# Edge stage of a graph-attention kernel: two operands of VectorE moved to PSUM, and the carried row added in two parts

## The chip, the cores and the metric

The kernel runs on one core of one Trainium2 chip. The metric is the device time of one launch in microseconds; the kernel before took 2041.8 us (median of three runs, 2036.73 to 2044.93).

## The reference

A graph-attention layer over N = 6250 nodes and E = 100000 edges, with a residual, and then a small network on the normalised result, again with a residual. The edges come sorted by `dst`. Cut to what matters:

```python
h = leaky_relu(layernorm(x) @ W.T + b)            # 6250 x 512, as 8 heads of 64
e_src, e_dst = sum(h * w_att_src), sum(h * w_att_dst)
e  = leaky_relu(e_src[src] + e_dst[dst])          # one score per edge and head
ex = exp(e - segment_max(e, dst)[dst])
a  = ex / segment_sum(ex, dst)[dst] * edge_attr_8
msg = h[src] * a[:, :, None]                      # 100000 x 512
x  = x + segment_sum(msg, dst)
x  = x + ffn(layernorm(x))                        # a decoder with two tiny networks
```

Everything is computed in float32; some operands are split into three bfloat16 parts that add up to the float32 value.

## The kernel before

Four stages run one after the other. `project` computes `h` and the scores for 49 tiles of 128 nodes and stores rows of 520 numbers (512 of `h` and 8 scores) in the HBM table `table_h`. `prepare` computes the node windows. `attend_windows` is the edge stage and holds the whole change. `finish` divides, normalises and runs the network.

The edge stage works on 112 groups of 7 x 128 = 896 edges. As `dst` is sorted, the edges of a group end in a window of 128 nodes that begins at the group's base. For a group g (slot s = g mod 3 of the triple buffers):

- ScalarE copies the 896 source node numbers to `src_idx` (`set_src`), and GpSimd issues seven indirect DMAs (L768), each of which gathers 128 rows of `table_h` into `gathered`. GpSimd does nothing else in this stage. It may refill a slot when the messages of three groups before are made (L766).
- VectorE, `make_member` (L778): compares the node numbers 0 to 127 (`node_no`, in SBUF) with the edges' place in the window (`rel`, in SBUF) and writes the 0/1 matrix `member16`, 128 x 896. TensorE transposes it (L872), ScalarE copies it widened to float32 (`widen_member`) and copies the transpose from PSUM (`turn_member`), both at L907.
- TensorE, `at_edges` (L863): fetches the destination scores of each edge by a product with the transposed matrix.
- VectorE, `scores` (L786 to L798): waits for the seven gathers, adds the scores. ScalarE takes the exponential (L919).
- VectorE, `messages`: L803 multiplies the exponentials by the edge attributes into `coef`, 128 x 56, in SBUF; L810 multiplies `gathered` (128 x 3584) by `coef`, each coefficient repeated over 64 columns, into `msg`.
- TensorE, `add_up` (L885): seven float32 products of `member` and `msg` accumulate the group's 128 x 512 sums in one of the PSUM banks 0 to 2 (each product is two matmul records), and L892 the sums of the exponentials in bank 3.
- ScalarE, `evacuate`, copies the sums to `summed`; VectorE, `evacuate_weights` (L830), the sums of the exponentials behind them.
- Windows overlap. So before the window is stored, SP loads the first row of it, as the groups before left it in `table_agg`, to `carry` (L752), VectorE adds it to row 0 of `summed` (`carry_in`, L840, one instruction of 1 x 520), and SP stores the 128 x 520 window (L741). The load waits until the store of the group before has landed.

Each engine has its own order, written out by hand as rounds: `stage(u, slot, lag, do)` runs step `do` for group u - lag in round u. VectorE's round is, in this order: `carry_in` (lag 4), `scores` (1), `make_member` (0), `weights_parts` (1), `messages` (1), `weights_last_part` (1), `evacuate_weights` (3). TensorE's is `at_edges` (1), `add_up` part 0 with three of seven products (2), `transpose` (0), `add_up` part 1 (2). SP's is window load (0), carry load (4), store (4). Rounds 0 to 8 and the last few are unrolled, those between run in a hardware loop of three rounds a pass. An engine waits in order: what stands behind a waiting instruction on its queue waits too.

Of the kernel before, what the change touches and what calls it, by code (L numbers as in the profile page):

```python
# [18 lines left out]
ALU = mybir.AluOpType  # L19
# [627 lines left out]
def attend_windows(nc, top, banks, t, keep, branch_semaphores):  # L647
# [6 lines left out]
    with ExitStack() as ctx:  # L654
# [22 lines left out]
        ex_rest = sb("w_ex_rest", [P, GROUP, HEADS])  # L677
        coef = sb("w_coef", [P, GROUP, HEADS])
        msg = sb("w_msg", [P, S3, GROUP, D])
# [4 lines left out]
        member_t = banks[4][:, :].bitcast(BF16)  # L684
        edge_dst = banks[6]

        s_no = sem("node_no_loaded")
        s_pool_on = sem("w_pool_went_on")
        s_i16 = sem("ident16_set")
# [32 lines left out]
        with nc.Block() as block:  # L722
            @block.sync
            def _(sp):
# [8 lines left out]
                def store(g, s):  # L733
                    base = sp.value_load(keep["bases_int"][0:1, bass.ds(g, 1)], min_val=0, max_val=NODES)
                    if isinstance(g, int) and g == 0:
                        sp.wait_ge(d["evac"], 1)
                        sp.wait_ge(d["evac_w"], 1)
                    else:

                        sp.wait_ge(d["carried"], g)  # L740
                    sp.dma_start(t["agg"][bass.ds(base, P), :], summed[:, s, :]).then_inc(s_put[s], 48)  # L741

                def load_carry(g, s):

                    if isinstance(g, int) and g == 0:
                        return
                    base = sp.value_load(keep["bases_int"][0:1, bass.ds(g, 1)], min_val=0, max_val=NODES)
                    if reused(g):
                        sp.wait_ge(d["carried"], g - 1)
                    before = (s - 1) % S3  # L750
                    sp.wait_ge(s_put[before], filled(g - 1, before, 48))
                    sp.dma_start(carry[:, :], t["agg"][bass.ds(base, 1), :]).then_inc(s_carry, 16)  # L752
# [21 lines left out]
            def _(dve):  # L774
                def make_member(g, s):
                    if old(g):
                        dve.wait_ge(d["sums"], g - 2)
                    nc.vector.tensor_tensor(  # L778
                        member16[:, s, :, :], node_no[:, :].unsqueeze(1).to_broadcast([P, GROUP, P]),
                        keep["rel"][:, bass.ds(g * GROUP, GROUP)].unsqueeze(2).to_broadcast([P, GROUP, P]),  # L780
                        ALU.is_equal).then_inc(d["member16"], 1)
# [19 lines left out]
                def messages(g, s):  # L801
                    dve.wait_ge(d["ex"], g + 1)
                    nc.vector.tensor_tensor(coef[:, :, :], ex[:, s, :, :],  # L803
                                            keep["dist"][:, bass.ds(g * GROUP, GROUP), :], ALU.mult
                                            ).then_inc(d["coef"], 1)
                    dve.wait_ge(d["coef"], g + 1)
                    if old(g):
# [4 lines left out]
                        gathered[:, s, :, 0:D].rearrange("p j (h d) -> p j h d", h=HEADS),  # L812
                        coef[:, :, :].unsqueeze(3).to_broadcast(shape), ALU.mult).then_inc(d["msg"], 1)

# [19 lines left out]
                def carry_in(g, s):  # L834
                    if isinstance(g, int) and g == 0:
# [3 lines left out]
                    dve.wait_ge(s_carry, 16 * g)  # L839
                    nc.vector.tensor_tensor(summed[0:1, s, :], summed[0:1, s, :], carry[:, :], ALU.add  # L840
                                            ).then_inc(d["carried"], 1)

                dve.wait_ge(s_no, 16)
                for u, slot in rounds(dve, 4):
                    stage(u, slot, 4, carry_in)
# [8 lines left out]
            def _(pe):  # L854
# [21 lines left out]
                def add_up(g, s, part):  # L876
                    if part == 0:
                        pe.wait_ge(d["msg"], g + 1)
                        pe.wait_ge(d["member"], g + 1)
                        if old(g):  # L880
                            pe.wait_ge(d["evac"], g - 2)
                    half = GROUP // 2
                    for j in range(half) if part == 0 else range(half, GROUP):
# [621 lines left out]
```

## Time and profile before

| | us |
|---|---|
| three runs | 2036.73, 2041.8, 2044.93 |
| median | 2041.8 |
| span of the profiled execution | 2022.8 |
| busy: PE / DVE / ACT / POOL | 1448.3 / 1285.9 / 488.2 / 1282.9 |
| mean granted TensorE clock | 0.864 of full speed |

PE is TensorE (PEld its weight loads), DVE is VectorE, ACT is ScalarE, POOL is GpSimd, SP is the engine that issues the plain DMAs (SPq its queue). The span runs from the first to the last instruction of one profiled execution; its device time is not listed apart from the three runs. An engine counts as busy while an instruction of its own runs, and that includes time in which the instruction is held up by something outside it. The edge stage takes the span from about 354 us to about 1738 us.

### The profile page before, as it was taken

What the parts mean: (1) busy time and instruction counts of PE and PEld (TensorE: products, weight loads), DVE (VectorE), ACT (ScalarE), POOL (GpSimd) and SP (SyncE); (2) the same over time, 40 slices, a digit from 0 to 9 for tenths busy, and PEclk for the clock granted to TensorE, in tenths of its full rate; (3) what the DMA queues carried; (4) which work ended last, traced back from release to release, by engine and by line L of the source; (5) the groups of instructions that cost most, each with busy time, mean ns of one, the idle gap of its engine ahead of it and who ended that gap; (6) DMA issues with size and microseconds to landing.
All of it is one profiled execution on the core that took longest, in us unless ns stands there. A gap on an engine that the chain in (4) does not pass through costs nothing. (4 is left out here: it accounts for less than half of the span.)

```text
span 2022.8 us, 23283 instructions
## 1 busy us (share of the span) xinstructions
PE 1448.3 (72%) x5502; PEld 680.4 (34%) x5502; DVE 1285.9 (64%) x2420; ACT 488.2 (24%) x1141; POOL 1282.9 (63%) x932
## 2 busy tenths in 40 slices
PE   5878782476677667677767677677676777189998
PEld 2333331233333233333333333333333333045555
DVE  5777875465665666655566555556665555588884
ACT  1222220222222222222222222222222222033332
POOL 1222221888888888888888888888888887023341
PEclk9899996688988988978797888888878888689988
DMA  6333333566566666566666556666655665325441
GB/s 222 126 126 126 126 126 65 158 179 180 174 175 179 185 177 175 170 179 176 180 179 176 170 170 181 179 176 178 177 171 171 180 180 164 121 105 187 169 154 67
DMA packets 151399, 326.43 MB, mean 161 GB/s; under 512 B 47313, under 2 KB 47569, under 8 KB 151247
## 3 DMA queue, kind: packets, MB, share of 16 engines
q0 software_dynamic: 62720, 208.78, 36.5%
q1 hardware_dynamic: 88654, 117.38, 16.9%
q8 instruction: 9, 0.15, 0.0%
q14 instruction: 16, 0.12, 0.0%
HBM read 255.82 MB, written 70.27 MB: 161 GB/s over the span
## 5 line engine op out<-in xcount | busy, mean ns | idle before, releaser
L768 POOL DMA_INDIRECT gathered<-table_h,w_src_idx x784 | 1121.0, 1430 | 256.4 <-issue 256.4
L885 PE MATMUL bank<-w_msg,member 128*128 128x512 f32 x1568 | 880.1, 710 | 1.8 <-DVE w_msg L810 1.8
L885 PEld LDWEIGHTS bank<-w_msg,member 128*128 128x128 f32 x1568 | 341.8, 231 | 367.3 <-issue 365.4
L810 DVE TENSOR_TENSOR w_msg<-gathered,w_coef 128x3584 f32<-128x3584 f32 x112 | 435.9, 3892 | 3.9
L786 DVE TENSOR_REDUCE at_dst<-bank 128x112 f32<-128x336 f32 x112 | 56.9, 508 | 525.2 <-DMA gathered<-table_h,w_src_idx 525.2
L872 PE MATMUL bank<-ident,member 128*128 128x128 bf16 x784 | 83.3, 265 | 421.6 <-DVE member L778 421.6
L919 ACT ACTIVATE w_ex<-w_diff 128x56 f32<-128x56 f32 x112 | 27.9, 249 | 967.8 <-DVE w_diff L798 967.8
L208 POOL TENSOR_TENSOR prod_dst<-hrow,w_dst 128x512 f32<-128x512 f32 x49 | 75.6, 1543 | 247.1 <-DVE hrow L237 247.1
L872 PEld LDWEIGHTS bank<-ident,member 128*128 128x128 bf16 x784 | 58.7, 117 | 513.4 <-DVE member L778 478.1
L277 PE MATMUL bank<-wt,xnT 128*128 128x512 f32 x392 | 199.7, 657 | 0.0
L1113 POOL TENSOR_TENSOR res<-x_in,y 128x2048 f32<-128x2048 f32 (+1 forms) x13 | 63.4, 4880 | 197.0 <-DMA out<-res 136.7
L1196 PE MATMUL bank<-h,w 128*128 128x512 f32 (+1 forms) x338 | 162.4, 625 | 0.0
L778 DVE TENSOR_TENSOR member<-node_no,k_rel 128x896 bf16<-128x896 f32 x112 | 121.8, 1087 | 10.6 <-DMA node_no<-in_node_no 10.6
L907 ACT ACTIVATE member<-member 128x896 f32<-128x896 bf16 x112 | 106.4, 950 | 64.6 <-DVE member L778 64.6
L277 PEld LDWEIGHTS bank<-wt,xnT 128*128 128x128 f32 x392 | 76.9, 206 | 93.6 <-issue 93.6
L907 ACT ACTIVATE memberT<-bank 128x896 bf16<-128x896 bf16 x112 | 100.7, 899 | 0.1
L840 DVE TENSOR_TENSOR summed<-summed,w_carry 1x520 f32<-1x520 f32 x111 | 76.4, 688 | 26.6 <-DVE summed L830 20.4
L286 PE MATMUL bank<-ident,xn 128*128 128x128 f32 x196 | 32.4, 289 | 78.3 <-DVE xn L227 78.3
L1196 PEld LDWEIGHTS bank<-h,w 128*128 128x128 f32 x338 | 64.0, 208 | 58.9 <-issue 56.9
L1142 ACT ACTIVATE h<-bank,b 128x512 f32<-128x512 f32 (+1 forms) x65 | 41.7, 661 | 133.3 <-PE bank L1196 67.1
L1207 PEld LDWEIGHTS bank<-w,h 128*128 128x128 f32 x490 | 64.5, 205 | 16.8 <-issue 16.1
L907 ACT ACTIVATE summed<-bank 128x512 f32<-128x512 f32 x112 | 65.8, 588 | 11.0 <-PE bank L892 11.0
(133 smaller groups left out, 1155.2 us busy)
## 6 DMA issues: line engine op xcount, KB each, us to landing
table_agg<-summed SPq DMA_DIRECT2D x112, 260.0 KB
table_agg<-zeros SPq DMA_DIRECT2D x50, 260.0 KB, 2.2
table_h<-hrow SPq DMA_DIRECT2D x49, 260.0 KB, 2.1
xt<-in_x SPq DMA_DIRECT2D x49, 256.0 KB, 2.7
gathered<-table_h,w_src_idx POOLq DMA_INDIRECT x784
agg_in<-table_agg SPq DMA_DIRECT2D x12, 1040.0 KB, 7.6
x_in<-in_x SPq DMA_DIRECT2D x12, 1024.0 KB, 5.5
out<-res SPq DMA_DIRECT2D x12, 1024.0 KB, 4.4
```

Of the source, the lines that this page charges most:

```text
L208: nc.gpsimd.tensor_tensor(prod_dst[:, s, :], hrow[:, s, 0:D], w_dst[:, :], ALU.mult).then_inc(s_pdst, 1)
L277: mm = nc.tensor.matmul(ps_h[s][:, :], xnT[:, s, c * P:(c + 1) * P], wt[:, c, :], start=False, stop=(c == DC - 1))
L768: pool.indirect_dma_start(out=gathered[:, s, j, :], out_offset=None, in_=t["h"][:, :], in_offset=bass.IndirectOffsetOnAxis(ap=src_idx[:, s ...
L778: nc.vector.tensor_tensor(member16[:, s, :, :], node_no[:, :].unsqueeze(1).to_broadcast([P, GROUP, P]), keep["rel"][:, bass.ds(g * GROUP, ...
L810: nc.vector.tensor_tensor(msg[:, s, :, :].rearrange("p j (h d) -> p j h d", h=HEADS), gathered[:, s, :, 0:D].rearrange("p j (h d) -> p j h ...
L840: nc.vector.tensor_tensor(summed[0:1, s, :], summed[0:1, s, :], carry[:, :], ALU.add).then_inc(d["carried"], 1)
L872: last = nc.tensor.transpose(member_t[:, j * P:(j + 1) * P], member16[:, s, j, :], ident16[:, :])
L885: nc.tensor.matmul(sums[s][:, :], member[:, s, j, :], msg[:, s, j, :], start=first, stop=final)
L907: return nc.scalar.activation(out, in_, ACT.Copy)
L1113: nc.gpsimd.tensor_tensor(res[:, s, 0:k, :], x[:, s, 0:k, :], y[:, s, 0:k, :], ALU.add).then_inc(d["res"], 1)
L1196: last = nc.tensor.matmul(bank[:, 0:w], w2[:, weights, :], h1[:, units, 0:w], start=(i == 0), stop=(i == len(pairs) - 1))
L1207: last = nc.tensor.matmul(y3[:, 8 * j:8 * j + 8], h2[:, g, j * P:(j + 1) * P], w3[:, g, :], start=(g == 0), stop=(g == 4))
```

## The change

The edge stage's `coef` and node numbers move from SBUF to PSUM banks 5 and 7, which the stage did not use. The node numbers are copied there once, by VectorE, before the rounds begin. `carry_in` becomes two instructions: the first adds `carry` to row 0 of the sums as they stand in their PSUM bank and writes columns 0 to 511 of row 0 of `summed`; the second adds the last eight columns as before. Each increments the semaphore `carried`, so it now counts two a group, and the waits on it are doubled. TensorE gets one more wait: before it overwrites a sums bank it waits for the `carry_in` of the group that had that bank. All other code is the same.

```diff
-        coef = sb("w_coef", [P, GROUP, HEADS])
+        coef = banks[5][:, 0:GROUP * HEADS].rearrange("p (j h) -> p j h", h=HEADS)
+        node_row = banks[7][:, 0:P]
+        s_row = sem("node_row_set")
@@ store(g, s), on SP
-                        sp.wait_ge(d["carried"], g)
+                        sp.wait_ge(d["carried"], 2 * g)
@@ load_carry(g, s), on SP
-                        sp.wait_ge(d["carried"], g - 1)
+                        sp.wait_ge(d["carried"], 2 * (g - 1))
@@ make_member(g, s), on VectorE
-                        member16[:, s, :, :], node_no[:, :].unsqueeze(1).to_broadcast([P, GROUP, P]),
+                        member16[:, s, :, :], node_row.unsqueeze(1).to_broadcast([P, GROUP, P]),
@@ messages(g, s), on VectorE
-                    nc.vector.tensor_tensor(coef[:, :, :], ex[:, s, :, :],
+                    nc.vector.tensor_tensor(coef, ex[:, s, :, :],
                                             keep["dist"][:, bass.ds(g * GROUP, GROUP), :], ALU.mult
                                             ).then_inc(d["coef"], 1)
...
                         gathered[:, s, :, 0:D].rearrange("p j (h d) -> p j h d", h=HEADS),
-                        coef[:, :, :].unsqueeze(3).to_broadcast(shape), ALU.mult).then_inc(d["msg"], 1)
+                        coef.unsqueeze(3).to_broadcast(shape), ALU.mult).then_inc(d["msg"], 1)
@@ carry_in(g, s), on VectorE
-                    nc.vector.tensor_tensor(summed[0:1, s, :], summed[0:1, s, :], carry[:, :], ALU.add
+                    nc.vector.tensor_tensor(summed[0:1, s, 0:D], sums[s][0:1, :], carry[:, 0:D], ALU.add
                                             ).then_inc(d["carried"], 1)
+                    nc.vector.tensor_tensor(summed[0:1, s, D:ROW], summed[0:1, s, D:ROW], carry[:, D:ROW], ALU.add
+                                            ).then_inc(d["carried"], 1)
 
                 dve.wait_ge(s_no, 16)
+                nc.vector.tensor_copy(node_row, node_no[:, :]).then_inc(s_row, 1)
+                dve.wait_ge(s_row, 1)
@@ add_up(g, s, part), on TensorE, part 0
                             pe.wait_ge(d["evac"], g - 2)
+                            if reused(g, S3 + 1):
+                                pe.wait_ge(d["carried"], 2 * (g - 3))
```

## Rows read from the trace of the kernel before

**Rows 1.** The page: busy time and shares by engine; POOL's busy tenths in 40 slices.
```profile
PE 1448.3 (72%) x5502; PEld 680.4 (34%) x5502; DVE 1285.9 (64%) x2420; ACT 488.2 (24%) x1141; POOL 1282.9 (63%) x932
POOL 1222221888888888888888888888888887023341
```
**Rows 2.** Stages: window, us, busy us of PE, PEld, DVE, ACT, POOL, clock, DMA, GB/s.
```profile
1000.00:1300.00 300.00, 212.63 (x873) 97.40 (x874) 179.64 (x271) 74.02 (x174) 247.73 (x172) 0.87 0.60 175
```
**Rows 3.** Waits from 440 to 1690 us: us in total, times, longest us.
```profile
DVE at_dst L786 <- DMA gathered<-table_h,w_src_idx: 471.0, 103, 5.7
```
**Rows 4.** Order of time, POOL: start us, us; first and last of 784 gathers.
```profile
354.49 1.82 POOL L768 DMA_INDIRECT gathered<-table_h,w_src_idx  x1 [17.77 <-issue]
...
1713.14 0.95 POOL L768 DMA_INDIRECT gathered<-table_h,w_src_idx  x1 [0.30 <-issue]
```
**Rows 5.** Order of time, DVE and POOL, one round of the loop.
```profile
1010.04 0.51 DVE L786 TENSOR_REDUCE at_dst<-bank 128x112 f32<-128x336 f32 x1 [4.19 <-DMA gathered<-table_h,w_src_idx]
...
1011.35 1.09 DVE L778 TENSOR_TENSOR member<-node_no,k_rel 128x896 bf16<-128x896 f32 x1
...
1012.11 1.16 POOL L768 DMA_INDIRECT gathered<-table_h,w_src_idx  x1 [0.30 <-issue]
...
1012.73 3.89 DVE L810 TENSOR_TENSOR w_msg<-gathered,w_coef 128x3584 f32<-128x3584 f32 x1
...
1013.57 3.88 POOL L768 DMA_INDIRECT gathered<-table_h,w_src_idx  x1 [0.30 <-issue]
...
1017.04 0.69 DVE L840 TENSOR_TENSOR summed<-summed,w_carry 1x520 f32<-1x520 f32 x1 [0.20 <-DVE summed L830]
...
1017.75 0.94 POOL L768 DMA_INDIRECT gathered<-table_h,w_src_idx  x1 [0.30 <-issue]
```
**Rows 6.** Order of time, a gather beside a reduction that reads PSUM alone.
```profile
416.86 0.51 DVE L786 TENSOR_REDUCE at_dst<-bank 128x112 f32<-128x336 f32 x1 [5.00 <-DMA gathered<-table_h,w_src_idx]
416.99 0.95 POOL L768 DMA_INDIRECT gathered<-table_h,w_src_idx  x1 [0.30 <-issue]
```
**Rows 7.** Order of time, the projection's POOL and DVE products side by side.
```profile
103.00 1.26 POOL L208 TENSOR_TENSOR prod_dst<-hrow,w_dst 128x512 f32<-128x512 f32 x1 [5.69 <-DVE hrow L237]
...
108.89 0.69 DVE L241 TENSOR_TENSOR prod_src<-hrow,w_src 128x512 f32<-128x512 f32 x1
...
108.94 1.77 POOL L208 TENSOR_TENSOR prod_dst<-hrow,w_dst 128x512 f32<-128x512 f32 x1 [4.68 <-DVE hrow L237]
...
109.62 0.69 DVE L244 TENSOR_REDUCE hrow<-prod_src 128x8 f32<-128x512 f32 x1
```
**Rows 8.** Lines L237 and L241: duration ns min/median/max, first and last start.
```profile
L237 DVE TENSOR_TENSOR hrow<-leak,bank x49: 677/686/690, 27.5 to 321.5; 128x512 f32<-128x512 f32 x49
L241 DVE TENSOR_TENSOR prod_src<-hrow,w_src x49: 691/692/1733, 28.2 to 322.2; 128x512 f32<-128x512 f32 x49
```
**Rows 9.** Groups of DVE, 460 to 1690 us: busy us, mean ns of one.
```profile
L803 DVE TENSOR_TENSOR w_coef<-w_ex,k_dist 128x56 f32<-128x56 f32 x101 | 21.1, 209 | 0.0
L830 DVE TENSOR_REDUCE summed<-bank 128x8 f32<-128x24 f32 x101 | 17.7, 175 | 0.0
```
**Rows 10.** Order of time, SP's queue and DVE: a store, carry loads, one awaited.
```profile
1006.03 0.42 SPq L741 DMA_DIRECT2D table_agg<-summed  x1
...
1009.34 0.28 SPq L752 DMA_DIRECT2D w_carry<-table_agg  x1
...
1728.08 0.28 SPq L752 DMA_DIRECT2D w_carry<-table_agg  x1
...
1729.86 0.69 DVE L840 TENSOR_TENSOR summed<-summed,w_carry 1x520 f32<-1x520 f32 x1 [4.14 <-DMA w_carry<-table_agg]
```
**Rows 11.** Order of time, PE: the products of two rounds.
```profile
1012.91 3.65 PE L885 MATMUL bank<-w_msg,member 128*128 128x512 f32 x8
...
1017.30 2.82 PE L885 MATMUL bank<-w_msg,member 128*128 128x512 f32 x6
...
1025.21 5.12 PE L885 MATMUL bank<-w_msg,member 128*128 128x512 f32 x8
```

## The prediction

> **What bounds the kernel now.** I read the page first. PE has the largest share, 72% of the span, but POOL stands at 8 tenths in every slice of the edge stage and at 1 to 4 elsewhere [rows 1], and the change lies in that stage alone. The stage's window row says more: in 300 us of it POOL is busy 247.73, PE 212.63, DVE 179.64, and the 16 DMA engines at 0.60 [rows 2]. Who waits for whom settles it: VectorE waits for the gathers 103 times in 103 rounds, 471.0 us in all [rows 3]. So the gathers come last, and everything behind them has slack.
>
> In the order of time POOL rests only 0.30 us between two gathers [rows 5]. 784 gathers start between 354.49 and 1713.14 us [rows 4]: 1358.65 / 783 = 1.735 us each, 12.15 us for a group of seven. An undisturbed one takes 0.95 + 0.30 = 1.25 us [rows 5]; seven would be 8.75. The missing 3.40 us are in two gathers of each round [rows 5]. One starts at 1013.57, while L810 runs from 1012.73 to 1016.62, and lasts 3.88 us instead of 0.95: it ends 0.83 us after L810 does. The other starts at 1012.11 inside L778 (to 1012.44) and lasts 1.16: it ends 0.83 us after L778 does. Two events with one law: a gather that needs something 0.12 us after its start gets it only when the VectorE instruction is through, and then needs 0.83 us more. Both instructions have two inputs in SBUF. A gather that starts inside L786, which reads PSUM alone, takes 0.95 [rows 6]: it isn't held. The projection shows the same of POOL's own arithmetic [rows 7]: L208 takes 1.26 us when it goes first, and 1.77 when it starts 0.05 us after L241 with its two SBUF inputs; L244, one SBUF input, runs inside that same L208 for its usual 0.69 and adds nothing. So two SBUF inputs hold GpSimd up, and one or none doesn't.
>
> **The change part by part.**
>
> *L810 reads `coef` from PSUM.* It then has one SBUF input. By the law above the blocked gather loses 3.88 - 0.95 = 2.93 us in every round. No row shows an instruction with one SBUF and one PSUM input beside a working GpSimd; the bounds are 0 (blocks as now) and 2.93 (does not). I take 2.93, as L244 with one SBUF input and L786 with a PSUM input both let GpSimd work.
>
> The Trainium skill, "SBUF — State Buffer", section "Who interferes with whom", says so outright: a Vector instruction with two SBUF inputs contends with a GpSimd instruction that reads SBUF, one with at most one SBUF input outside the two-port modes does not. The trace agrees as far as it goes (3.88 against 0.95 us).
>
> *L778 reads the node numbers from PSUM.* Likewise one SBUF input. Of the 3.40 us, 2.93 are L810's; the rest, 0.47 us a round on average, is L778's (0.21 in the round shown), and it goes too, between 0 and 0.47. I take all of it.
>
> *What still blocks.* Six VectorE instructions a round of some 0.21 us (L790, L793, L798, L818, L803 [rows 9], L823), and the new last part of `carry_in`, keep two SBUF inputs. A gather's critical instant falls into one of them with a chance of 0.21 / 1.25 and then waits 0.1 us on average: 7 x 0.017 = 0.12 us a round. So POOL needs 8.75 + 0.12 = 8.87 us a round (8.75 to 9.1).
>
> *VectorE's own time.* A round's chain goes from L786 at 1010.04 to the end of L840 at 1017.73: 7.69 us of 12.15 [rows 5]. L810, L778 and L840 change an operand to PSUM. L237, 128 x 512 with one input in PSUM, takes 686 ns, and L241 with both in SBUF 692 when undisturbed [rows 8]: 0 us each. Both operands are read repeatedly (64 columns a coefficient, seven times the node row); no row shows that from PSUM, nearest is L786, which walks 336 elements of PSUM with a stride in 0.51 us [rows 6] where L237 needs 0.69 for 512, so the same slope. I take 0; the other bound is a doubled rate, which is a rival below. L803 writes to PSUM: its 209 ns [rows 9] could become 0.1 us more or less. `carry_in` becomes 512 columns (0.68, as L237) plus eight (0.175 as L830 [rows 9], to 0.21): +0.17 to +0.2 us. Sum: 7.9 us, up to 8.2. That is under 8.87, so it is hidden, but the cover shrinks from 4.2 us to 0.7 to 1.0 us: if VectorE's round grew beyond 8.87 each 0.1 us would cost 11 us.
>
> The Trainium skill, "VectorE: DVE Perf Modes", section "The TRN2 errata", gives 120 fixed cycles for a PSUM source against 58 for an SBUF one. By that three instructions a round would cost 65 ns more each, 0.2 us, and VectorE's round would be 8.1 us, still under POOL's. The row on L237 shows no such cost, and the row decides.
>
> *The new wait on TensorE* (part 0 of `add_up` g for `carry_in` g - 3). Queued behind it are all products, the transposes, and through them VectorE. But the same place already waits for the messages of g, which VectorE makes in the same round as `carry_in` g - 3 and 6 us later. It costs 0.
>
> *The doubled count on SP.* The store waits for the second part: 0.2 us later. Behind it on SP's queue stand the next window load, the carry load and the next store. Store to carry load is 3.3 us, the load's landing about 1.8 (1728.08 to 1729.86, where VectorE waited for it) [rows 10], `carry_in` with its handover about 1.1: some 6.2 us of 8.87. Cost 0, cover 2.6 us, from which slower transfers would take.
>
> *The copy of the node numbers*: once, at most 0.5 us.
>
> *Sum.* 783 x (1.735 - 8.87 / 7) = 783 x 0.468 = 366 us. Fill and drain around the 784 gathers, and the stages before and after, stay. Span 2022.8 - 366 = 1657; around it lie 19 us (2041.8 - 2022.8), so 1676 us for a run like the median.
>
> **What is late next.** Three things come close to 8.87 us a round.
> DMA: 0.60 x 12.15 = 7.3 us of all 16 engines a round [rows 2], a share of 0.82 afterwards. PE: 212.63 / 300 x 12.15 = 8.6 us a round, but at a mean clock of 0.87 [rows 2]. Eight records took 3.65 us in one round and 5.12 in the next [rows 11], after products had ended at 1020.12 and PE had stood nearly idle for over 4 us. At the full clock (2.4 GHz) the work is 8.6 x 0.87 = 7.5 us. With a round of 8.87 only about 1.4 us of idleness is left, so I expect the clock to rise. VectorE: 7.9.
>
> **The rivals.**
> (a) *TensorE or the DMA engines become the bound.* If the clock stays at 0.87 and PE keeps some 0.6 us of waits (for L778's output and L830), the round is 8.6 + 0.6 = 9.2 us; if packets stretch by a third under the denser load, 7.3 becomes 9.8. For: both would stand at over 0.8. Against: neither is at its limit on average, and the three slots let POOL run up to two groups ahead of a late round. Times: 9.2 gives 2041.8 - 112 x 2.95 = 1711; 9.8 gives 1779.
> (b) *The lock doesn't care where the second input lies.* Any two-input instruction, PSUM or not, holds GpSimd. Then POOL's 12.15 stays, and the 0.2 us more on VectorE are hidden: 2042. For: no row shows the mix. Against: rows 6 and 7.
> (c) *Slower: PSUM delivers a repeated operand at half the rate.* An element costs 1.045 ns ((3.89 - 0.69) / (3584 - 520), rows 5), so L810 would take 3.75 us more and L778 0.94; VectorE's round is then 7.69 + 0.2 + 4.69 = 12.58 us, and it, not POOL, is the bound: 112 x 0.43 = +48 us, 2090. It decides from the point where the two take over 4.26 us more in sum. Against: L237 and L786 at the usual rate.
>
> **How the numbers follow.** Forecast (round 8.75 to 9.1) 0.66, rival (a) 0.22, (b) 0.08, (c) 0.04. Range: from 8.7 us a round, 1656, up into rival (a) at 9.8 us, 1780; that leaves out (b), (c) and the far end of (a), about 0.17. Less than 0.5% (10 us) can't be told from no change with this kernel. Faster 0.88, same 0.08, slower 0.04.
>
> **What would show it.** In the new profile no gather should last over 1.2 us, the mean of a gather should fall from 1.43 (1.735 - 0.30) to about 0.97 us, and POOL's tenths should fall slightly while its gathers come every 1.27 us. L810 should stay at 3.89 and L778 at 1.09. VectorE's wait for the gathers should shrink from 4.5 us to under 1 a round, and PE's clock should rise above 0.9. I am wrong if gathers of 3.9 us are still there (b), if L810 is longer (c), or if POOL shows waits for `msg` or VectorE waits for TensorE instead of the gathers (a).

## The result, and the profile after

The changed kernel took 2155.1 us (median of 4, 2149.2 to 2164.6) where the kernel before takes 2042.8 (4 runs, 2036.7 to 2044.9): ratio 1.058, 95% interval 1.052 to 1.063. The forecast was 1676 us. Run again, unaltered, in two later sets of runs on two different chips, the changed kernel took 2111.6 us in one and **1664.9 us** in the other, each beside runs of the kernel before at 2045.5 and 2039.0. The record names the chips of the later sets, but not that of the first measurement, nor the one on which the kernel before was profiled. So this section shows two profiles of one program: "the first" is that of the 2155 us, "the later" that of the 1665 us. Line numbers are those of the changed kernel: L770 is the gather, L812 the messages, L780 the member comparison, L788 the first reduction of a round, L842 and L844 the carried row, L743, L733 and L754 SP's store, window load and carry load.

The pages, first and then later: busy time and shares, and POOL's and the DMA engines' tenths of 40 slices.

```profile
PE 1415.2 (66%) x5502; PEld 665.2 (31%) x5502; DVE 1289.2 (60%) x2532; ACT 493.6 (23%) x1141; POOL 902.0 (42%) x932
POOL 1222223554645545545545445445445454122331
DMA  5333335565645645655555555555555455324441
```
```profile
PE 1327.7 (80%) x5502; PEld 617.2 (37%) x5502; DVE 1294.2 (78%) x2532; ACT 488.4 (29%) x1141; POOL 905.2 (54%) x932
POOL 1222222237777777777777777777777712133341
DMA  6433343258888888888888888888888843244431
```

POOL's busy time fell from 1282.9 us [rows 1] to 902 in the first and 905 in the later: the hold of GpSimd by VectorE is gone in both. What is left is spread differently: 7 tenths in nearly every slice of the stage in the later profile, 4 to 6 in the first one, where POOL now waits. The 300 us windows of [rows 2] say it again, first and then later (busy us of PE, PEld, DVE, ACT, POOL, then clock, DMA share, GB/s):

```profile
1000.00:1300.00 300.00, 189.35 (x803) 86.01 (x804) 167.67 (x277) 69.89 (x163) 148.32 (x157) 0.83 0.56 159
```
```profile
1000.00:1300.00 300.00, 252.53 (x1196) 112.07 (x1194) 249.44 (x410) 101.22 (x238) 227.14 (x240) 1.00 0.83 244
```

The gathers (duration in ns min/median/max, first and last start) and what POOL waited for, in the first profile and then in the later one:

```profile
L770 POOL DMA_INDIRECT gathered<-table_h,w_src_idx x784: 940/946/1297, 353.9 to 1825.0; - x196
its engine sat idle before it (us, times) until:
  DVE w_msg L812: 359.6, 35
  issue: 235.6, 711
  ACT w_src_idx L915: 152.7, 38
```
```profile
L770 POOL DMA_INDIRECT gathered<-table_h,w_src_idx x784: 942/949/1297, 357.4 to 1339.5; - x196
its engine sat idle before it (us, times) until:
  issue: 227.0, 690
  ACT w_src_idx L915: 28.7, 94
DMA to landing us min/median/max: 3.5/3.9/4.9
```

No gather lasts 3.9 us any more in either. But in the first profile POOL stood still 35 times until VectorE's messages had freed a slot, 359.6 us in all, and VectorE in turn waited before L788 (first, then later):

```profile
L788 DVE TENSOR_REDUCE at_dst<-bank x112: 487/506/509, 365.5 to 1835.2; 128x112 f32<-128x336 f32 x112
its engine sat idle before it (us, times) until:
  remote: 419.7, 38
  PE bank L869: 72.4, 33
```
```profile
L788 DVE TENSOR_REDUCE at_dst<-bank x112: 507/508/509, 369.0 to 1344.4; 128x112 f32<-128x336 f32 x112
its engine sat idle before it (us, times) until:
  DMA gathered<-table_h,w_src_idx: 139.5, 112
```

"Remote" is a release for which the trace has no event at the right time. Before, this wait was for the gathers [rows 3]; in the later profile it still is, 1.2 us a time. In the first one most of it is for TensorE, which had long been done. The second round shows it best, since up to it the two executions do the same. Order of time, first profile:

```profile
368.84 0.91 ACT L915 ACTIVATE memberT<-bank 128x896 bf16<-128x896 bf16 x1
...
369.80 0.46 PE L869 MATMUL bank<-window,memberT 128*128 128x48 bf16 x7 [1.01 <-ACT memberT L915]
...
379.06 0.51 DVE L788 TENSOR_REDUCE at_dst<-bank 128x112 f32<-128x336 f32 x1 [6.95 <-remote]
...
381.38 0.93 PE L878 MATMUL bank<-ident,member 128*128 128x128 bf16 x7 [3.85 <-issue]
...
393.81 0.92 ACT L915 ACTIVATE memberT<-bank 128x896 bf16<-128x896 bf16 x1 [11.36 <-remote]
```

and later profile:

```profile
372.31 0.91 ACT L915 ACTIVATE memberT<-bank 128x896 bf16<-128x896 bf16 x1
...
373.28 0.46 PE L869 MATMUL bank<-window,memberT 128*128 128x48 bf16 x7 [1.01 <-ACT memberT L915]
...
377.72 0.51 DVE L788 TENSOR_REDUCE at_dst<-bank 128x112 f32<-128x336 f32 x1 [2.13 <-DMA gathered<-table_h,w_src_idx]
...
380.12 0.55 PE L878 MATMUL bank<-ident,member 128*128 128x128 bf16 x7
...
381.01 0.90 ACT L915 ACTIVATE memberT<-bank 128x896 bf16<-128x896 bf16 x1
```

The seven L869 end at 370.26 in the first profile. The semaphore that VectorE waits for is recorded as raised at 378.97, 8.7 us later (later profile: products end at 373.74, raised at 373.75). Not all of that is lost, as VectorE also needs the gathers: it stood idle 6.95 us instead of 2.13. L878's products end at 382.31, and ScalarE starts on them at 393.81, 11.5 us later (later profile: 0.34 us). This is all or nothing: in 35 of the 112 rounds of the first profile L788 starts 12.0 to 13.1 us after the end of its L869 products, in 68 under 1 us. The gathers' transfers, by contrast, aren't late: from the start of a gather to the end of its last packet it is 3.76 us in the median of the first profile and 3.85 in the later one. A third thing is late: SP. Its own register instructions and DMA issues, which take 0.02 to 0.5 us elsewhere, take 0.70 us each in many cases while gathers stream. In the first profile, order of time on SP's queue and POOL:

```profile
1029.03 0.95 POOL L770 DMA_INDIRECT gathered<-table_h,w_src_idx  x1 [0.30 <-issue]
1029.34 0.71 SPq L743 DMA_DIRECT2D table_agg<-summed  x1
...
1032.79 0.95 POOL L770 DMA_INDIRECT gathered<-table_h,w_src_idx  x1 [0.30 <-issue]
1036.39 0.00 SPq L733 DMA_DIRECT2D window<-table_shifts  x1
1036.65 0.51 DVE L788 TENSOR_REDUCE at_dst<-bank 128x112 f32<-128x336 f32 x1 [11.51 <-remote]
...
1043.99 0.95 POOL L770 DMA_INDIRECT gathered<-table_h,w_src_idx  x1 [10.26 <-DVE w_msg L812]
```

Between the store at 1029.34 and the window load at 1036.39 SP waits for nothing that is late; it works through its register instructions (start us, us; the first three took 0.03 to 0.04 us each at 1018.4 us, ahead of a slow stretch):

```
1034.28 0.697  L732 register arithmetic
1034.98 0.697  L733 wait for edge_dst, by a register
1035.68 0.698  L733 move
1036.39 0.002  L733 DMA issue
```

The last gather is issued at 1032.79, SP's slow stretch ends at 1036.39, and at 1036.65 VectorE wakes too, 12.6 us after the L869 products it waited for (1023.67 + 0.33). In the meantime POOL has used up its two groups of lead, and waits for VectorE in turn until 1043.99. That comes about once in three groups and makes the mean round (1824.99 - 353.90) / 783 x 7 = 13.15 us, against 12.15 before. POOL's two waits above, 359.6 + 152.7 us in 112 rounds, come to 4.6 us a round (the usual gaps of 0.30 us in them included); they are the difference to the 8.75 us that seven gathers take alone.

One number sorts the executions. The trace records each raise of a semaphore by a DMA queue ("landing"), here counted by stage, beside SP's register and issue instructions of 0.6 to 0.8 us between 354 and 1800 us (value loads left out):

```
                              landings, 0-345 us   whole run   slow SP instr.
kernel before (its profile)        2520             19823           0
the change, first profile          2520              7381         458
the change, later profile          2520             19832           0
```

Up to the first gather all agree; from there the first profile lacks most of the landings that the other two have, from the first group on. It also lacks some of the raises by engines: 4492 are recorded, against 5811 in the later profile of the same program.

### The profile page after: what moved, and what is told of

It is laid out like the page before. It is cut to its first block and busy times, and to the rows that moved or that the text cites. A ratio compares the mean times of both kernels' runs of the same rounds, so it can differ in the third digit from the quotient of the medians.

```text
span 2156.6 us, 23605 instructions
## 1 busy us (share of the span) xinstructions
PE 1415.2 (66%) x5502; PEld 665.2 (31%) x5502; DVE 1289.2 (60%) x2532; ACT 493.6 (23%) x1141; POOL 902.0 (42%) x932
## 5 line engine op out<-in xcount | busy, mean ns | idle before, releaser
L770 POOL DMA_INDIRECT gathered<-table_h,w_src_idx x784 | 741.5, 946 | 747.9 <-DVE w_msg L812 359.6
L893 PE MATMUL bank<-w_msg,member 128*128 128x512 f32 x1568 | 817.3, 667 | 1.8 <-DVE w_msg L812 1.8
L812 DVE TENSOR_TENSOR w_msg<-gathered,bank 128x3584 f32<-128x3584 f32 x112 | 435.3, 3887 | 3.8
L893 PEld LDWEIGHTS bank<-w_msg,member 128*128 128x128 f32 x1568 | 315.7, 214 | 324.4 <-issue 320.3
L878 PE MATMUL bank<-ident,member 128*128 128x128 bf16 x784 | 77.8, 253 | 508.1 <-DVE member L780 470.9
L788 DVE TENSOR_REDUCE at_dst<-bank 128x112 f32<-128x336 f32 x112 | 56.1, 501 | 511.1 <-remote 419.7
L878 PEld LDWEIGHTS bank<-ident,member 128*128 128x128 bf16 x784 | 56.5, 113 | 602.6 <-DVE member L780 481.5
L1204 PE MATMUL bank<-h,w 128*128 128x512 f32 (+1 forms) x338 | 175.0, 666 | 0.0
L842 DVE TENSOR_TENSOR summed<-bank,w_carry 1x512 f32<-1x512 f32 x111 | 75.3, 679 | 155.9 <-ACT summed L915 91.9
L780 DVE TENSOR_TENSOR member<-bank,k_rel 128x896 bf16<-128x896 f32 x112 | 121.6, 1085 | 0.0
L869 PE MATMUL bank<-window,memberT 128*128 128x48 bf16 x784 | 38.5, 185 | 74.7 <-ACT memberT L915 66.5
L1215 PEld LDWEIGHTS bank<-w,h 128*128 128x128 f32 x490 | 70.6, 221 | 21.1 <-issue 20.3
L1150 ACT ACTIVATE h<-bank,b 128x512 f32<-128x512 f32 (+1 forms) x65 | 41.6, 661 | 152.7 <-PE bank L1215 84.7
```

The lines of the kernel that those rows point to most:

```text
L770: pool.indirect_dma_start(out=gathered[:, s, j, :], out_offset=None, in_=t["h"][:, :], in_offset=bass.IndirectOffsetOnAxis(ap=src_idx[:, s ...
L780: nc.vector.tensor_tensor(member16[:, s, :, :], node_row.unsqueeze(1).to_broadcast([P, GROUP, P]), keep["rel"][:, bass.ds(g * GROUP, GROUP ...
L812: nc.vector.tensor_tensor(msg[:, s, :, :].rearrange("p j (h d) -> p j h d", h=HEADS), gathered[:, s, :, 0:D].rearrange("p j (h d) -> p j h ...
L842: nc.vector.tensor_tensor(summed[0:1, s, 0:D], sums[s][0:1, :], carry[:, 0:D], ALU.add).then_inc(d["carried"], 1)
L878: last = nc.tensor.transpose(member_t[:, j * P:(j + 1) * P], member16[:, s, j, :], ident16[:, :])
L893: nc.tensor.matmul(sums[s][:, :], member[:, s, j, :], msg[:, s, j, :], start=first, stop=final)
```

## The experiments

18 runs in six sets; all kernels of a set ran on one chip, and no two sets on the same. The expectations speak of theories: A, gathers that nothing holds up come too densely and keep wakings and SP back; B, the split carried row is the cost; C, the node numbers in PSUM; D, the load of the DMA engines; E and G, something else than the stream of gathers; H, the chip that a run is on. In the tables "landings" is the count of recorded landings in the run's profile, "slow SP" the count of SP instructions as above, and "round" is 7 x (last - first gather) / 783. Line numbers shift by a few between kernels.

### Set 1: the parts alone, and less lead

```diff
e1  coef in PSUM; node_no and the carried row as before
e2  node numbers in PSUM; coef and the carried row as before
e3  the carried row in two parts, with its waits; coef and node_no as before
e4  the whole change, and
-                        wait_alone(pool, d["msg"], g - 2, s_pool_on)
+                        wait_alone(pool, d["msg"], g - 1, s_pool_on)
```

> Of the change only the coefficients lie in PSUM; node numbers and the carried row are as before. Theory A (gathers that nothing holds up run too far ahead and too densely, and wakings by semaphores and SP's instructions then come late): the 3.89 us multiply no longer holds up a gather, so the gathers of a group run at 1.25 to 1.28 us and the stall comes as with the whole change: 2100 to 2170 us, SP instructions of 0.70 us in its records, gather rounds near 13 us. Theory B (the split carried row with its doubled count and TensorE's added wait is the cost): those are absent, so the gain forecast appears, 1680 to 1780 us. Theory C (the node numbers in PSUM are the cost): likewise 1700 to 1800 us.

> Only the node numbers lie in PSUM. Theory A: the held-up gather beside the member comparison goes from 1.16 to 0.95 us, 112 times 0.2 us, so at most 24 us of gain and no stall, as the multiply still holds up a gather each round: 2018 to 2045 us. Theory C: 2100 us or more. Theory B: 2018 to 2045 us.

> Only the carried row is added in two parts, the first read from PSUM, with the doubled count and TensorE's added wait. Theory A: nothing that holds up a gather goes, and the round is still GpSimd's 12.15 us: 2035 to 2050 us. Theory B (this is what costs): 2100 us or more. Theory C: 2035 to 2050 us.

> The whole change, and the gathers of group g wait for the messages of group g-2 instead of g-3, so that GpSimd runs at most one group ahead and pauses once a round instead of once in three rounds. Theory A: no long stretch of gathers without a pause, so the late wakings are short and the round becomes VectorE's 7.9 us plus the waits between the last landing of a group and its scores, or some 10 to 11 us: 1800 to 1920 us. Theory B or C (the split row, PSUM operands, or anything else in VectorE's or TensorE's chain): the pace of the gathers was not the limit, and one buffer less of lead makes it slower: 2155 to 2250 us.

```
              us (median)   ratio, 95% interval      landings   slow SP
e1 coef       2005.2        0.985 (0.980 to 0.989)     8809       202
e2 node       2026.2        0.994 (0.992 to 0.996)     9642         3
e3 carry      2036.2        0.998 (0.996 to 1.001)     9908        20
e4 less lead  2135.9        1.050 (1.044 to 1.057)     7343       365
```

e2 and e3 came as theory A had it, and show no cost of these two parts while the gathers are still held: 13 us of gain for e2, none for e3. e1 fell between: too slow for B and C, too quick for A, and its four runs lie wide apart (1992.8 to 2046.3). Its trace stalls as the change does, but still lets L778 hold up a gather now and then (a row of its waits, us in total, times, longest; and its gathers):

```profile
ACT memberT L907 <- remote: 267.4, 45, 9.3
...
L768 POOL DMA_INDIRECT gathered<-table_h,w_src_idx x784: 940/946/1869, 357.8 to 1656.9; - x196
```

Why holds of up to 0.9 us should bring 150 us against the whole change isn't settled. e4 missed the ranges of all theories: with one group less of lead the stall stays, and POOL, which was to pause briefly in each round, stops 72 times for 9.5 us in the median. All four have under 10,000 landings, e2 and e3 too, which kept the 3.9 us hold and didn't stall. They lack raises by engines too (4247 and 4437 recorded), so missing records alone don't make a kernel late.

### Set 2: spacing, bytes, rows, stores

```diff
e5  the whole change, behind each gather (pause is a new tile)
+                        wait_alone(pool, s_pause, g * GROUP + j, s_pool_on)
+                        nc.gpsimd.memset(pause[:, 0:8], 0.0).then_inc(s_pause, 1)
e6  in the 102 groups of the hardware loop: out=gathered[:, s, j, 0:260], rows of 260 columns read
e7  in the same 102 groups: out=gathered[0:64, ...], ap=src_idx[0:64, ...]
e8  in the 102 stores of the hardware loop: summed[:, s, 504:520] instead of all 520 columns
```

> The whole change, and behind each gather GpSimd writes 8 columns of a tile that nobody reads, and waits for that write before the next, so that the gathers start further apart than 1.25 us. Theory A (a stream of gathers with nothing between them keeps TensorE's and the DMA queues' wakings and SP's instructions back): with 0.1 to 0.3 us between gathers the 0.70 us SP instructions go or become rare, and a round costs 7 gathers of 1.4 to 1.55 us, 10 to 10.9 us: 1800 to 1900 us. Theory D (not the spacing, but the mean load of the DMA engines delays them): at a tenth or two less load little changes, 2080 to 2150 us. Theory E (the pace of the gathers is unrelated to the late wakings): 2155 us or more.

> The whole change, with gathers of 260 columns instead of 520 in all but the first nine groups (the tables' rows are then wrong ones, the count of gathers, of their rows and of their semaphore increments stays). Theory A (what matters is how densely GpSimd issues): same pace of issue, so the stall stays: 2100 to 2160 us and over 300 SP instructions of 0.70 us. Theory D (the bytes that the DMA engines move): the share of the engines in dense stretches falls from 0.8 to about 0.5 and the stall goes: 1670 to 1780 us.

> The whole change, with gathers of 64 rows instead of 128 in all but the first nine groups (half of the output rows of each are then stale); the count of gathers stays, bytes and row descriptors halve. If the number of descriptors written or moved is what delays, the stall goes: 1670 to 1780 us, or less if a gather of half the rows is also issued faster. If it is each gather's fixed part (its instruction, its increments from the 16 queues), the stall stays: 2100 us or more.

> The whole change, with stores of 16 columns instead of 520 in all but the first nine groups (the sums of a window are then not stored). Theory D (load of the DMA engines): 266 KB of 2.1 MB less a round, a gain of up to an eighth of the stall: 2000 to 2100 us; if the store's transfer was on the path of the carried row, the same. Theory A: 2130 to 2160 us, as the gathers are as dense as before.

```
                us (median)   ratio, 95% interval      landings   slow SP
e5 8 columns    2139.6        1.047 (1.044 to 1.051)     7342       423
e6 half bytes   2109.9        1.032 (1.026 to 1.037)     6823       384
e7 half rows    2122.7        1.038 (1.031 to 1.046)     7007       446
e8 small store  2134.8        1.044 (1.040 to 1.048)     7590       349
```

e5 tested nothing: the write fits into the gap that each gather leaves anyway, and the gathers still start 1.26 us apart (order of time of e5):

```profile
1012.54 0.96 POOL L772 DMA_INDIRECT gathered<-table_h,w_src_idx  x1 [0.18 <-POOL pause L778]
1013.50 0.12 POOL L778 MEMSET pause<- 128x8 f32 x1
1013.80 0.95 POOL L772 DMA_INDIRECT gathered<-table_h,w_src_idx  x1 [0.18 <-issue]
```

The other three leave out part of the data, so their results are not the layer's; their times tell what the transfers weigh. They rule out theory D: the DMA engines' tenths in the edge stage fall from 5 or 6 to 2 or 3 in e6 and e7, and neither half the bytes, nor half the rows, nor nearly no stores takes the stall away. They come 20 to 45 us under the change's first time, about as much as that kernel's own two stalled times differ (2155 and 2112).

### Set 3: real pauses, and the split row undone

```diff
e9   the whole change, once in each group
+                        if j == 3:
+                            if not (isinstance(g, int) and g == 0):
+                                wait_alone(pool, s_pause, g, s_pool_on)
+                            nc.gpsimd.memset(pause[:, 0:1560], 0.0).then_inc(s_pause, 1)
e10  the same with 3120 columns
e11  as e5 with 512 columns
e12  coef and node_row in PSUM, the carried row as before:
-                    nc.vector.tensor_tensor(summed[0:1, s, 0:D], sums[s][0:1, :], carry[:, 0:D], ALU.add
...
+                    nc.vector.tensor_tensor(summed[0:1, s, :], summed[0:1, s, :], carry[:, :], ALU.add
                                             ).then_inc(d["carried"], 1)
```

> The whole change, and once in each group, behind the fourth gather, GpSimd writes 1560 columns of a tile that nobody reads: by the 0.53 us of the 520 columns before (rows of L201) some 1.6 us. Theory A (what starves the wakings is an unbroken stream of gathers): a pause of 1.6 us every 8.75 us lets the late events through, the round is 8.75 + 1.4 = 10.2 us where the pause is long enough: 1800 to 1880 us; if 1.6 us doesn't suffice, 2050 to 2150 us. Theory G (the stream is not the cause; it is what VectorE's and TensorE's chains do with their operands in PSUM): 2155 us or more.

> The same with 3120 columns, some 3.2 us, about as long as the multiply of the kernel before held up a gather. Theory A: the round is 8.75 + 3 = 11.8 us with no stall, and few SP instructions of 0.70 us: 1980 to 2040 us, faster than the whole change although GpSimd is given more to do. Theory G: 2200 us or more, as GpSimd works longer and the stall stays.

> The whole change with 512 columns written behind each gather, some 0.5 us, of which 0.3 us lies in the gap that each gather leaves anyway: gathers start 1.45 to 1.55 us apart. Theory A with any small gap sufficing: a round of 10.2 to 10.9 us, 1800 to 1900 us. Theory A with a long gap needed: the stall stays at 2100 to 2160 us, and only the pauses help. Theory G: 2160 us or more.

> Coefficients and node numbers in PSUM, the carried row added as before, in one instruction with both operands in SBUF. Theory A: nothing of 3.9 or 1.1 us holds up a gather any more, the 0.69 us row of one partition at most: the stall stays, 2080 to 2160 us. Theory B (the split row and its waits make the stall once the gathers are fast): 1680 to 1900 us.

```
                 us (median)   ratio, 95% interval      landings   slow SP   round
e9  1.42 us      1801.4        0.884 (0.880 to 0.888)     19830        1     10.04
e10 2.72 us      1947.5        0.956 (0.947 to 0.964)     19799        2     11.34
e11 0.54 us x7   1986.1        0.975 (0.971 to 0.979)     19791        2     11.70
e12 no split     1661.8        0.817 (0.813 to 0.821)     19827        1      8.79
```

Three of the four missed their ranges: e10 came 32 us under its own, as the write took 2.72 us and not 3.2; e11 86 us over, as its gathers start 1.66 us apart and not 1.5; e12 18 us under that of theory B.

By these alone one would write: pauses cure the stall, and the split row is its cause, since e12 has no pause whatever between its gathers and is the quickest of all. The second is wrong, and the first isn't shown by this set. e12's first 16 us of the edge stage are the same instructions as the change's, no carried row has been touched by then, and yet the change's landings are already missing there. And all four of this set have their landings complete. What the four share isn't an edit but the chip, and the hour at which they ran.

### Set 4: the same three kernels on another chip

No edits: e13 is the changed kernel, e14 is e12, e15 is e9.

> The whole change, not altered, on this run's chip, beside two kernels that were fast on the chip before. Theory H (the late wakings belong to the chip that a run is on: the semaphore landings of the edge stage are recorded in full, some 19,800, on the chip on which all four kernels were fast, and 6,800 to 9,900 on the chips on which the others were slow, already in the first gathers, where the kernels do the same): on a chip with full landings the change runs at 1650 to 1690 us; on a chip with few, at 2140 to 2165 us. Theory B (the split row makes the stall): 2140 to 2165 us on every chip.

> The change without the split of the carried row, not altered from its first run. Theory H: 1650 to 1690 us on a chip with full landings, 2080 to 2165 us on one with few. Theory B: 1655 to 1675 us on every chip.

> The whole change with one pause of 1.6 us in each group, not altered from its first run. Theory H: 1795 to 1810 us on a chip with full landings; on one with few it says nothing of the pause: if the pause helps there, below 2050 us, if not, 2130 to 2180 us. Theory A with B (a pause mends the stall that the split row makes): 1795 to 1810 us on every chip.

```
                 us (median)   ratio, 95% interval      landings   slow SP   round
e13 the change   2111.6        1.033 (1.029 to 1.037)      7473      396     12.73
e14 as e12       2149.6        1.052 (1.048 to 1.056)      7094      370     12.90
e15 as e9        1920.4        0.940 (0.936 to 0.943)      8953      219     11.11
```

e13 stalls as theories B and H both had it, but 28 us under their range. e14 decides against the split row: one kernel, 1661.8 us in one set and 2149.6 in the other, 29% apart, while the kernel before stayed at 2036.8 and 2045.5. The kernel without the split row stalls too. The waits of L788 in e12 and in e14 (idle us, times, until):

```profile
  DMA gathered<-table_h,w_src_idx: 148.4, 112
```
```profile
  remote: 510.2, 49
  PE bank L867: 71.2, 49
```

e15 shows that a pause of 1.42 us in each group takes a large part of the stall away where there is one: a chip with few landings costs 1920 - 1801 = 119 us with it, against 2112 - 1665 = 447 without (e16 below). Of the three versions that ran on both kinds of chip it is the one that beat the kernel before on both, by 6% and by 12%.

### Sets 5 and 6: the change on a chip with full landings, and the long pause

No edits: e16 is the changed kernel, e17 and e18 are e10.

> The whole change, not altered, on whatever chip this set runs on. Theory H (the chip decides): with some 19,800 landings recorded 1650 to 1690 us, with under 10,000 recorded 2105 to 2165 us, and nothing between. If a chip with full landings gives 2100 us or more, the split row has a part in it after all.

> The whole change with one pause of 3.2 us in each group, not altered from its first run (1947.5 us, on the chip with full landings). On a chip with full landings 1930 to 1965 us again. On one with few: if a pause as long as the multiply's old hold lets all late wakings through, 1930 to 1975 us and under 30 SP instructions of 0.70 us; if the length of the pause is not what counts, a stall beside it, 2000 to 2150 us.

> The whole change with one pause of 3.2 us in each group, not altered (1946 and 1948 us in two sets, both on chips with full landings). On a chip with few landings: if a hold of 3 us a group, as the multiply gave in the kernel before, lets the late wakings through, 1935 to 1980 us and under 30 SP instructions of 0.70 us; if the hold is not what spared the kernel before, 2000 to 2150 us. On a chip with full landings 1930 to 1965 us, which would tell nothing new.

```
                 us (median)   ratio, 95% interval      landings   slow SP   round
e16 the change   1664.9        0.818 (0.809 to 0.827)     19832        0      8.78
e17 as e10       1946.2        0.956 (0.943 to 0.970)     19806        0     11.34
e18 as e10       1949.1        0.958 (0.948 to 0.968)     19798        0     11.34
```

e16 is the later profile shown above: the changed kernel itself is fast where the landings are complete, as theory H had it. e17 and e18 both fell on chips with full landings and repeat e10. Whether a pause of 2.7 us cures the stall on the other kind was not seen. That the kernel before didn't stall there, and e2 and e3 with its 3.9 us hold didn't, speaks for it. The kernel before has no profile from a set that stalled; that it runs on both kinds of chip is known by its times alone (medians of 2032.8 to 2045.5 over all sets).

The six sets fell three and three: full landings in sets 3, 5 and 6, few in sets 1, 2 and 4, every profile of a set alike. Each chip was seen once, so that it is the chip, and not the time at which a set ran, is the plainest reading and no more; where this text says "kind of chip", it stands for both.

## Why the prediction was right and wrong

**What held, on chips with full landings.** The result there, 1664.9 us, lies in the range (1656 to 1780) and 11 us under the forecast. Term by term from the later profile:
- *L810 and L778 no longer block.* Forecast 2.93 + 0.47 us a round. No gather lasts over 1.30 us, and the two terms together are right. Their split isn't: in e2, where the node numbers alone lie in PSUM, the gather that L810 holds waits 3.36 us (2.92 in the profile before, means of 111), and the round only goes from 12.15 to 12.10 us. What L778 no longer holds, L810 then does. Rival (b) is out: an instruction with one input in SBUF and one in PSUM doesn't hold up a gather, on either kind of chip.
- *What still blocks.* Forecast 0.12 us; a round takes 982.1 / 783 x 7 = 8.78 us, so 0.03 over 8.75. Only the stage's first gather takes over 1.0 us: none is seen to be held by the short instructions with two SBUF inputs.
- *VectorE.* Forecast an unchanged 3.89 and 1.09 us and a carried row of 0.85 to 0.89 in two parts (0.75, as they overlap a little). Its wait for the gathers was to fall under 1 us a round and fell to 1.2 (139.5 / 112). The order of time of one round:

```profile
1007.86 0.68 DVE L842 TENSOR_TENSOR summed<-bank,w_carry 1x512 f32<-1x512 f32 x1 [0.20 <-DVE summed L832]
...
1008.47 0.14 DVE L844 TENSOR_TENSOR summed<-summed,w_carry 1x8 f32<-1x8 f32 x1
1008.78 0.42 SPq L743 DMA_DIRECT2D table_agg<-summed  x1
...
1009.75 0.51 DVE L788 TENSOR_REDUCE at_dst<-bank 128x112 f32<-128x336 f32 x1 [1.14 <-DMA gathered<-table_h,w_src_idx]
...
1010.92 1.08 DVE L780 TENSOR_TENSOR member<-bank,k_rel 128x896 bf16<-128x896 f32 x1
...
1012.05 0.22 DVE L805 TENSOR_TENSOR bank<-w_ex,k_dist 128x56 f32<-128x56 f32 x1
...
1012.30 3.89 DVE L812 TENSOR_TENSOR w_msg<-gathered,bank 128x3584 f32<-128x3584 f32 x1
1013.04 0.28 SPq L754 DMA_DIRECT2D w_carry<-table_agg  x1
```

  No operand in PSUM costs anything, repeated or not, so rival (c) is out. The prediction's estimate of 0.2 us for three PSUM sources, worked out from the cycle counts of the Trainium skill's page "VectorE: DVE Perf Modes" (section "The TRN2 errata"), doesn't show either: 3.89 us stand as before and 1.08 against 1.09 [rows 5].
- *What is late next.* DMA share 0.83 (forecast 0.82); PE 252.53 / 300 x 8.78 = 7.4 us a round at clock 1.00 (forecast 7.5 at the full clock). The clock did rise, and rival (a) didn't come: the round is 8.78 us with both at their computed load.
- *The stages around stay.* From the last gather's end to the end of the span it is 2022.8 - 1714.1 = 308.7 us in the profile before and 326.3 in the later one, with TensorE at a lower clock there. The 100 us with PE at 100.00 us busy, before and then later (columns as in the 300 us windows, clock third from the end):

```profile
1834.00:1934.00 100.00, 100.00 (x407) 57.29 (x407) 87.97 (x286) 33.91 (x65) 40.87 (x42) 0.93 0.46 162
```
```profile
1460.00:1560.00 100.00, 100.00 (x378) 55.77 (x377) 82.86 (x272) 32.79 (x61) 34.72 (x35) 0.88 0.44 161
```

  That isn't a cost of the change. The same stretch behind the last gather is 316.2 us in e2 and 327.7 in e3, whose edge stage runs as before, and 330.7 in the first profile, where TensorE was far from full load; over all traces it lies between 308.7 and 339.7, and the profile before has the shortest. Why the clock falls more in one execution than in another isn't shown.
- *The 19 us around the span.* No run shows this term: the device time is 1.8 to 1.9 us over the span in every run. The rest of the 19 us is that the profile before came from an execution some 17 us quicker than the median. As the forecast added it back, it is sound as a step from median to median: 2041.8 - 376.5 (gained in the gathers, forecast 366) = 1665.3, and 1664.9 was measured.

**What failed, where the change was measured.** The step is the sum itself: it set a round to the 8.87 us that POOL needs, and priced every handover around it as the trace of before shows it. The round came out at 13.15 us, with POOL idle in the difference, and 2155.1 us were measured instead of 1676. The sentence "everything behind them has slack", the 0 for TensorE's side and the 0 for SP's queue "with a cover of 2.6 us" all rest on wakings that come at once (0.01 us in the later profile) and on SP instructions of 0.02 to 0.5 us. In four of seven measurements (the first and sets 1, 2 and 4) that held only for kernels in which a long hold interrupts the gathers. Without it a waking can take up to 13.1 us (TensorE to VectorE; 11.5 us from TensorE to ScalarE), longer than a whole round of 8.78. One such comes in about every third round, POOL uses up its lead of two groups meanwhile, and stops (10.26 us in the stretch shown). No rival had a mechanism of this kind: (a) looked for a full engine, and in the first profile no engine is full. The one clause of "what would show it" that fired, POOL waiting for `msg` and VectorE for TensorE, was put down to (a), and that reading was wrong: L812 was late because VectorE had been woken late.

Could it have been seen? The one profile at hand had its landings complete and no SP instruction slow. Nothing in it points to the other kind. A chance of 0.04 for "slower", resting on one profile of one chip, was too small. The mechanism of the gain was right on both kinds of chip; that a denser stream of gathers could make the handovers late had no place in the range.

**What stays open.** Why wakings are late. The transfers themselves keep their pace, bytes, rows and stores matter little (e6 to e8), a pause does (e15 against e13). It also stays open whether the recording of the run takes part: every run told of here was made with a record of its own (each has a granted clock), none without. In the slow kernels the missing records and the late instructions come in the same stage; but e2 and e3 lack the records too (9642 and 9908 landings) and aren't late. The Trainium skill's page "NOTIFIC — Programmer's Manual", section "When the ring fills", says that a full queue of event records drops the new record, overwrites the oldest or stalls the engine that makes them, as it is set. The trace would fit the first (7381 landings of 19832, and the earliest 2520 all there), but nothing here shows that a queue was full, nor whether a stall of the third kind is what holds SP and the wakings.

## What to carry to other kernels

An engine that is freed raises the rate of everything it issues, and a forecast that only adds up busy times takes for granted that semaphores and the engines' instruction streams keep up: give "the handovers get slower" its own share of the range. Before an edit is blamed for a time, run the edited and the unedited kernel on more than one chip and at more than one time, and compare a count that should be equal in all (here the recorded landings): the first three sets of this study would have blamed a harmless line. Where this kernel must not lose on either kind of chip, a short pause in the stream of gathers (e9 and e15: 1801 and 1920 us) is the safer version of those measured, at 8% over the best. Before two executions are compared by one profile each, see how far the unchanged stages differ between them: here by up to 31 us.

## What the runs showed that was not expected

- The same program on two chips: 1664.9 and 2111.6 us, with the kernel before at 2039.0 and 2045.5. In six sets the two kinds came three times each.
- On the chips with few landings, in the kernels that stall, SP's plain register instructions take 0.70 us each during a stream of gathers, in the first profile mostly (93%) from 3.5 us after the stream's first gather, and in the stretch shown to 3.6 us after the start of its last.
- A gather over 64 rows holds POOL 0.90 us against 0.95 for 128: nearly all of it is fixed.
- A write of 8 columns fits for nothing into the 0.30 us between two gathers; one of 512 columns (0.54 us) puts them 1.66 us apart.
